# Gate and up products of a gated decoder as seven quarter products, in two passes over the tokens

## What is computed

```
x = x + tanh(g_xattn[1]) * xattn(layernorm(x), ctx, ctx, ...)       # "lane attention"
x = x + tanh(g_ffn[1])   * ffn(layernorm(x), gate_w, up_w, down_w, gate_a, ..., down_b)

def _matmul_lora(x, w, a, b, scale=1.0):
    out = jnp.einsum('bsd,hd->bsh', x, w)
    return out + jnp.einsum('bsr,hr->bsh', jnp.einsum('bsd,rd->bsr', x, a), b) * scale
gate = _matmul_lora(x, gate_w, gate_a, gate_b)
up = _matmul_lora(x, up_w, up_a, up_b)
hidden = jax.nn.silu(gate) * up
out = _matmul_lora(hidden, down_w, down_a, down_b)
```

## Time and profile before

| | us |
|---|---|
| median of three runs | 3377.55 |
| lowest and highest | 3376.01, 3385.93 |
| the profiled execution, its own time | 3380.17 |
| its span in the profile | 3378.5 |
| `swiglu_ffn`: from its first transfer | 1863.5 |
| first product of gate and up | 1885.7 |
| first down product | 2871.4 |

### The profile page before, as it was taken

The page is one execution under the profiler, slowest core; times in us unless marked ns, Lnnn a source line. Parts: engine busy times, 40 slices in busy tenths (PEclk is TensorE's granted clock), DMA queues, the critical chain, the costliest instruction groups (busy, mean ns, idle before and its releaser), DMA issues. The chain is left out here.

```text
span 3378.5 us, 52215 instructions
## 1 busy us (share of the span) xinstructions
PE 3192.5 (94%) x20893; PEld 2452.0 (73%) x20893; DVE 1420.9 (42%) x1993; ACT 889.7 (26%) x1218; POOL 346.4 (10%) x302
## 2 busy tenths in 40 slices
PE   7999979987599989999998799999999999999999
PEld 6788846655377866666666688888888888777877
DVE  3111158876888747877885312121222122200000
ACT  2222233322333335554553211111111111200000
POOL 0000020000000023323331110101111100000000
PEclk9999989999799989999999899999999999999999
DMA  5334357774522132212221522222222223643443
GB/s 184 116 112 146 114 148 141 152 180 89 215 76 76 57 128 84 86 74 87 87 87 44 184 96 95 96 95 100 89 100 92 95 93 132 210 144 97 140 145 103
DMA packets 351086, 387.41 MB, mean 115 GB/s; under 512 B 155344, under 2 KB 262480, under 8 KB 349024
## 3 DMA queue, kind: packets, MB, share of 16 engines
q1 hardware_dynamic: 347488, 382.50, 35.7%
q10 hardware_dynamic: 3456, 2.90, 0.3%
HBM read 228.85 MB, written 147.96 MB: 112 GB/s over the span
## 5 line engine op out<-in xcount | busy, mean ns | idle before, releaser
L2357 PE MATMUL g_ps<-g_xs,g_wt 128*128 128x512 f32 x4128 | 948.6, 390 | 0.0
L2357 PEld LDWEIGHTS g_ps<-g_xs,g_wt 128*128 128x128 f32 x4128 | 774.5, 188 | 159.7
L2416 PE MATMUL g_ps<-g_wd,g_h 128*128 128x512 f32 x2016 | 464.6, 393 | 7.7 <-DVE g_act_out L2273 4.1
L2416 PEld LDWEIGHTS g_ps<-g_wd,g_h 128*128 128x128 f32 x2016 | 382.0, 190 | 89.8 <-DVE g_act_out L2273 4.5
L2273 DVE SCALAR_TENSOR_TENSOR g_act_out<-g_ps,g_g,g_act_out 128x512 f32<-128x512 f32 (+1 forms) x88 | 66.1, 752 | 672.7 <-ACT g_act_out L2206 672.6
L2206 ACT ACTIVATE g_act_out<-g_ps 128x512 f32<-128x512 f32 (+1 forms) x88 | 52.6, 597 | 634.4 <-PE g_ps L2357 634.3
L1368 PE MATMUL kv_gps<-kv_xh,kv_wh 128*128 128x512 f32 x512 | 205.6, 401 | 1.0 <-DVE kv_xl L1265 1.0
L1368 PE MATMUL kv_gps<-kv_xh,kv_wl 128*128 128x512 f32 x512 | 201.0, 393 | 0.0
L1368 PE MATMUL kv_gps<-kv_xl,kv_wh 128*128 128x512 f32 x512 | 200.7, 392 | 0.0
L945 PE MATMUL f_gps<-f_xt,f_qwh 128*128 128x256 f32 x1024 | 193.5, 290 | 1.4 <-DVE f_xt L840 1.4
L2146 POOL TENSOR_TENSOR g_wt<-g_raw,g_wt 128x1024 fp32r<-128x1024 f32 x43 | 102.8, 2391 | 853.9 <-ACT g_wt L2183 853.9
(11 more groups left out here) (248 smaller groups left out, 4210.0 us busy)
## 6 DMA issues: line engine op xcount, KB each, us to landing
g_h<-g_hidden SPq DMA_DIRECT2D x176, 256.0 KB, 2.7
g_hidden<-g_h SPq DMA_DIRECT2D x84, 512.0 KB, 2.7
kv<-kv_y SPq DMA_DIRECT2D x16, 1024.0 KB, 5.7
early_x<-x SPq DMA_DIRECT2D x32, 512.0 KB, 6.2
g_down<-g_raw SPq DMA_DIRECT2D x22, 512.0 KB, 2.8
g_raw<-g_down SPq DMA_DIRECT2D x22, 512.0 KB, 4.5
g_raw<-in_L_ffn_gate_w_dram SPq DMA_DIRECT2D x21, 512.0 KB, 3.9
g_raw<-in_L_ffn_up_w_dram SPq DMA_DIRECT2D x21, 512.0 KB, 3.9
```

Source lines behind the costliest of these rows:

```text
L2357: w = pe.matmul(gps[:, c % 2, m, :], wt[m][i][:, l, ks], xs[c][:, r, k, :], start=(k == 0 and a == 0), stop=(k == NK - 1 and a == 2))
L2416: w = pe.matmul(to, tile[:, p % RING, l, cols], wd[f][:, r, os], start=(f == 0 and a == 0), stop=False)
```

## The change

**Quarter products.** The product of (gate, up) with all tokens is cut in two on three sides: gate and up are the two weight rows, features 0 to 511 and 512 to 1023 are the two halves of the sum, and batches of even and odd number are the two token columns. Eight quarter products (12 matmuls each) become seven, by sums of blocks on both sides. The seven right factors are kept in SBUF for 1024 tokens, each 512 features x 512 tokens, split: B11, B21, B22 are quarters of the normalized rows, T1 to T4 are differences of them. The seven left factors are quarters of the weights and four sums (`sums`), for each hidden block.

**Two passes.** Seven factors for 1024 tokens take 14 of 21 slots of SBUF, so the tokens go in two passes of 1024. A unit `u` is one hidden block in one pass (44 units). In pass one the merged gate and up weights are also stored (`g_merged`), and pass two loads them from there; the down weights are merged in pass two. At the change of pass (unit 21, the narrow one, and unit 22) the 28 rows of the second pass are turned.

```
+    B11, B21, B22, T1, T2, T3, T4 = range(7)
+    FACTORS = (B11, T2, B21, T3, T1, T4, B22)
+    LAST_FACTORS = ((B11, 1, 0), (B11, 0, 0), (T1, 1, 0), (B21, 0, 1), (B22, 1, 1))
+    ORDER = (FACTORS, (T2, T3, T4, B11, T1, B21, B22))
+    NB = 6
...
+            def first_sums(u):
+                dve.tensor_tensor(sums[0][:, :], raw[1][:, 0:512], raw[1][:, 512:D], ALU.add).then_inc(S["sum"], 1)
+                dve.tensor_tensor(sums[1][:, :], sums[0][:, :], raw[0][:, 0:512], ALU.subtract).then_inc(S["sum"], 1)
+            def second_sums(u):
+                dve.tensor_tensor(sums[2][:, :], raw[0][:, 0:512], raw[1][:, 0:512], ALU.subtract).then_inc(S["sum"], 1)
+                dve.tensor_tensor(sums[3][:, :], raw[0][:, 512:D], sums[1][:, :], ALU.subtract).then_inc(S["sum"], 1)
...
+            def first_and_sixth(u):
+                dve.wait_ge(S["m1"], full(u) + 1)
+                dve.wait_ge(S["m"], products(u) + 2)
+                dve.tensor_tensor(u2, ps[:, bank(u, 1), :], m1, ALU.add).then_inc(S["u2"], 1)
...
+            def three(u, to, q, j, first, last, turns):
+                turns = list(turns)
+                for k in range(KH):
+                    if turns:
+                        turn(turns.pop(0))
                     for a, (l, r) in enumerate(((0, 0), (0, 1), (1, 0))):
-                        w = pe.matmul(gps[:, c % 2, m, :], wt[m][i][:, l, ks], xs[c][:, r, k, :],
-                                      start=(k == 0 and a == 0), stop=(k == NK - 1 and a == 2))
+                        w = pe.matmul(ps[:, bank(u, to), :], wq[q % NQ][:, l, P * k:P * k + P], xs[j][:, r, k, :],
+                                      start=(first and k == 0 and a == 0), stop=(last and k == KH - 1 and a == 2))
+                w.then_inc(S["m"], 1)
...
+            def load_raw(u):
+                f = u % NF
+                if u:
+                    sp.wait_ge(S["wl"], quarters(u))
+                    sp.wait_ge(S["mst"], 32 * u if u <= LAST else 32 * LAST + 16)
...
+            for n in range(9, 17):
+                load_row(n)
+            load_raw(1)
+            for n in range(17, 28):
+                load_row(n)
...
+            for n in range(40, 48):
+                load_row(n)
+            load_raw(NF + 1)
+            for n in range(48, 56):
+                load_row(n)
```

**Lane attention.** The normalized rows of two batches are kept (`yn[0]`, `yn[1]`), GpSimd forms four differences for each pair, two batches later, and `x3n` has seven rows of 512 for each token pair:

```
+            def row_sum(pair, i):
+                if i == 0:
+                    pool.wait_ge(S["yn"], 2 * pair + 2)
+                    if not isinstance(pair, int) or pair:
+                        pool.wait_ge(S["trout"], 16 * pair)
+                else:
+                    pool.wait_ge(S["tr"], 4 * pair + i)
...
+                pool.tensor_tensor(tr[:, i, :], a, b, ALU.subtract).then_inc(S["tr"], 1)
...
+                    if par == 0 and c >= 3 and c < 7 and (not isinstance(b, int) or b >= 4):
+                        row_sum(b // 2 - 2 if isinstance(b, int) else pair - 2, c - 3)
...
             power(B - 2)
+            for i in range(4):
+                row_sum(B // 2 - 2, i)
             power(B - 1)
+            for i in range(4):
+                row_sum(B // 2 - 1, i)
```

More of the change, by code:

```diff
@@ L1938, in pieces, with batch @@
+        def batch(q, t):
+            return 8 * (q // 2) + 2 * t + q % 2
         def pieces(tile):
             return tile[:, :].rearrange("p (k h) -> p k h", h=P)
[L1941 to L1955 removed]
@@ new lines, in high, with high_sum @@
+            def high(u, m, a, k, nth):
+                q = quarters(u) + k
+                if u <= LAST:
+                    act.wait_ge(S["wa"], added(u) + nth)
+                else:
+                    act.wait_ge(wld[m], raw_loaded(u, m))
+                act.copy(place_free(q), raw[m][:, 512 * a:512 * a + 512]).then_inc(S["wh"], 1)
+            def high_sum(u, i, k):
+                act.wait_ge(S["sum"], 4 * full(u) + i + 1)
+                act.copy(place_free(quarters(u) + k), sums[i][:, :]).then_inc(S["wh"], 1)
@@ new lines, in silu_odd, with high_hidden @@
+            def silu_odd(u):
+                if narrow(u):
+                    act.wait_ge(S["m"], products(u) + 5)
+                    act.wait_ge(S["hf"], 2 * u)
+                    act.activation(u2[P - REST:P, :], ps[0:P - REST, bank(u, 1), :], ACT.Silu).then_inc(S["sgb"], 1)
+                else:
+                    act.wait_ge(S["c12"], full(u) + 1)
+                    act.activation(u2, u2, ACT.Silu).then_inc(S["sgb"], 1)
+            def high_hidden(u, e):
+                c = e
+                rows = slice(P - REST, P) if narrow(u) else slice(0, P)
+                act.wait_ge(S["hf"], 2 * u + e + 1)
+                if u:
+                    act.wait_ge(hst[c], stored(u))
+                act.copy(h[rows, 2 * c:2 * c + 2, 0, :], hf[rows, c, :].rearrange("p (a t) -> p a t", a=2)).then_inc(S["hh"], 1)
@@ L2236, in _ @@
-            blocks(act, step)
-            for f in range(8, NF):
+                act.copy(to, raw[f % 2][:, :]).then_inc(S["wh2"], 1)
+            high(0, 0, 0, 0, 1)
+            high_x(0, 1, 2, 3)
+            high_sum(0, 1, 1)
+            high(0, 0, 1, 2, 3)
+            high_x(4, 5, 6, 7)
+            first_product(0)
+            high_sum(0, 2, 3)
+            high_x(8, 9, 10, 11)
+            high_sum(0, 0, 4)
+            high_x(12, 13, 14, 15)
+            high(0, 1, 1, 5, 4)
+            high_sum(0, 3, 6)
@@ new lines, in bank_free, with product @@
+            def bank_free(u, k):
+                n = quarters(u) + k - NB
+                if n < 0:
+                    return
+                v = next(v for v in range(NU) if n < quarters(v + 1))
+                k = n - quarters(v)
+                if narrow(v):
+                    pe.wait_ge(S["hf"], 2 * v + k + 1)
+                else:
+                    pe.wait_ge(S[("m1", "u2", "c11", "u3", "c22", "c21", "c12")[k]], full(v) + 1)
+            def product(u, k, turns=()):
+                bank_free(u, k)
+                q = quarters(u) + k
+                pe.wait_ge(S["wl"], q + 1)
+                x_there(u, FACTORS[k])
+                three(u, k, q, FACTORS[k], True, True, turns)
```

940 lines of the change are left out of this document (579 added, 361 removed).

## The result

The changed kernel takes 3349.15 us (median of four runs, 3347.45 to 3350.69), the kernel before 3381.74 (median of four, the three in the table above among them, 3376.01 to 3388.39). The ratio is 0.990, 95% interval 0.988 to 0.9925: about 33 us faster, where 76 were forecast (3302 us, range 3282 to 3340). The sign was right, and the size was less than half.

The account below looks back on a forecast made before the run. TensorE was taken to bound the last stage. From 3377.6 us, -108.8 + 4 - 3 + 21 + 7 + 0 + 4 = -75.8 gave 3302 us, range 3282 to 3322, upper end stretched to 3340 by rivals.

Parts of the forecast that it names:

- The rate of a product and the number of products: Gate and up products: 4128 matmuls become 3648 at an unchanged 0.2267 us each, -108.8 us.
- rival 4: Products run slower than 0.2267 because straight-line code replaces a loop: at 0.25, +85 us, no change; chance 0.02.
- rival 3: VectorE becomes the bound: a unit is 23.5 us, +157 us, 3459 us, slower than before; chance 0.04.
- Lane attention: GpSimd's added subtractions hide in idle time, 0; the tail's four subtractions and larger last store cost +7 us (5 to 9).
- The ring: Raw weights in pass one, load to last low part: 17.9 us a round against 20.0, so 0 for steady units.
- six low parts at 1.2 = 7.2: Step in the raw weights' round in pass one: GpSimd's six low parts in a row take 7.2 us.
- a rival, at 0.16: Raw weights' round exceeds 20 us in pass one as VectorE sums wait for GpSimd: +30 us, 3332 us; chance 0.16.
- Unit 20: Last full unit of pass one, counted among the steady units: 0, upper bound +1.5 us a unit.
- Unit 2: Early pass one, stretch from unit 1 to unit 2: no extra time, 0.
- First unit and change of pass: Turning 28 rows at each place: +4 us (-6 to +12) at the first, +21 us (11 to 35) at the second.
- Start of the down products: Waits of about 2 us at the first piece and 9 at the fifth, 11 as before: 0 (-6 to +8).
- Clock: Lower granted clock after two new waits of 5 to 8 us: +4 us (0 to 8).

Follow-up runs that it names:

- experiment 12: Changed kernel with separate gate and up loads, earlier clearing, rows ahead of weights, later residual rows, and lane-tail sums on VectorE with store ahead: 3308.74 us.
- experiment 3: Changed kernel with rows 17 to 27 and 48 to 55 loaded ahead of the next unit's weights in SyncE's queue: 3336.60 us.
- experiment 5: Changed kernel with VectorE's last two sums for units 2 to 20 reading one operand from PSUM, not SBUF: 3343.67 us, one run.
- experiment 1: Changed kernel with next gate weights loaded after the third low part and four sums, up weights after the sixth low part: 3337.99 us.

## Why the prediction missed

**Right.** The rate of a product and the number of products: pass two runs at 19.49 us a unit, as in the text, and straight-line code costs nothing there (rival 4 is out). VectorE is not the bound of a unit (rival 3 is out: its queue was the same when the units fell to 20.04). Lane attention itself costs nothing and its end +8.6 against +7: four sums of 1.3 as forecast, 1.3 for the longer last store against 1.6, and 2.0 us more for a store of the pair before that stood behind the last result. I had said that this pair costs nothing because its sums lie beside the projection. They do; its store doesn't.

**The ring** (+7.2 where I had 0). The failed step is "six low parts at 1.2 = 7.2". They took 9.4. I had a row in which the two engines hinder each other (1.43 for 0.81, though of a VectorE operation with one tile and two columns as inputs, not of the form of the sums) and used it only for a rival, at 0.16. With 9.4 the 17.9 become 20.1, and the up weights landed in 5.2 to 6.1 us where the sum has 5.5: 19.8 to 20.7. The ring came out at 20.4 against 20.0 and not at 21.5, so it cost a quarter of that rival's price. The margin of 2 us should have been worked out with the low parts as slow as that row hinted.

**Unit 20** (+6.7 where I had 0). I counted the clearing as nothing and didn't ask what stands behind the load that waits for it. It is 0.14 us of work that moved a store, a load and an addition by six.

**Unit 2** (+9.3 where I had 0). The prediction let the ring start in step. It starts late: unit 1's additions need the two banks in which rows are turned and run at 1944 to 1948 us, just when unit 1 begins, and the chain then goes round the ring at its full length:

```profile
1953.57 7.16 POOL g_wq L2242 x5
1960.74 0.40 SPq L2078
1961.18 5.30 DMA g_raw<-in_L_ffn_up_w_dram
```

TensorE stood 6.2 us from 1961.1 and then ran slower for a while: the 48 matmuls behind it took 13.28 us in place of 10.9 (granted clock 0.59 from 1967 to 1975 us). The released loads took off 4.1 (2.8 in experiment 12); that the rest goes with the banks was not tried.

**First unit and change of pass** (+10.5 for +4, +28.4 for +21). Both mechanisms were right and both sums too small. With the waits for rows gone (experiment 3), the six products with rows took 34.1 us and not 30.0: 6.6 the first, part of it at the lower clock, and 5.45 to 5.66 the others where I had 5.0. From there to unit 1's third product it took 3.6 over the pure time, where I had 2.6. The wait for row 17 cost 9.4 with what follows it (8 forecast), that for row 48 3 to 6 (4.7). At the change of pass a row costs 0.8 us even without a wait for memory ((56.5 - 33.1) / 28), where the forecast's 16 us for 28 rows made it 0.58: VectorE's sums and hidden low parts stand between the rows in the chain, and beside GpSimd they took 1.67 to 1.79 us. What they cost there was not tried alone.

**Start of the down products** (+6.6 for 0). "About 2 us at the first piece and 9 at the fifth" was nearly right (3.5 and 10.2), but it isn't "11 as before": before, the standstill was 7.5 us, and what my 11 held beyond that was clock, which a longer wait costs again. I set a wait against a sum of wait and clock. From the last product to the end of the first quarter it takes 138.9 us where it took 132.3. Of these 6.6 us, 1.6 aren't the start's: the last matmuls of the quarter took 0.72 us in place of 0.43 from 2973.5 on, in a stretch with a granted clock of 0.76 (2969 to 2978 us).

**Clock** (+4 forecast). It has no row of its own. What lower clock cost stands in the rows of the waits that it followed: 1.1 us in the first turn and three matmuls behind row 17, 2.4 us behind unit 2's wait, and part of the change of pass and of the down products.

## What to carry over

When a change makes an engine's stretch shorter, work out every ring that comes within some 2 us of the new unit (17.9 against 20.0 here) with the durations that its members have beside each other, not alone; a GpSimd operation beside VectorE sums over SBUF costs both. For every load or store that gets a new wait, write down the whole queue behind it: the row loads, the store of the merged weights in unit 20, the store of pair 6 and the fifth piece of the hidden state each stood in SyncE behind something that they had nothing to do with, and for each a change of order took away most of the wait (at the fifth piece 3.4 of 8.7 us came back at the ninth). Releasing a buffer by halves, each at its own last reader, is cheap slack for such a ring.

## What the hardware showed

- VectorE with both operands in SBUF and GpSimd slow each other down by up to a whole instruction: 0.69 us became up to 1.78, 1.29 became 1.74, and one PSUM operand on VectorE's side ended it (0.68, beside low parts of 1.30).
- After a standstill of 7.8 us the turn took 1.11 us and not 0.63 and three matmuls 1.28 and not 0.70, that is 0.427 us each against 0.2267 in the steady stretch, TensorE at its lower level of 1.2 GHz (granted clock 0.50 from 1926 to 1929 us). At row 48, behind a wait of 3.2 us (busy for 3.8 of the 7 us from 2400 on), it was the same (1.08 and 1.28, granted clock 0.50 from 2407 to 2412), so a short wait is dearer than it reads.
- A 512 KB load of up weights landed 5.2 to 6.1 us after its issue with the gate load issued just ahead of it (units 3 to 20; up to 6.7 in experiment 5), and 3.8 to 4.1 us after it when the gate load had gone out 4.1 us earlier (experiment 1).
